# Attention inside a four-layer kernel: one projection per turn, its halves swapped by DMA, and the maxima turned by 128 stationary columns

## The reference

```python
def _rope(q, k, seq_len, head_dim):
    ...
    def rot(t):
        t = t.reshape(*t.shape[:-1], half, 2)
        t0, t1 = (t[..., 0], t[..., 1])
        r0 = t0 * cos - t1 * sin
        r1 = t1 * cos + t0 * sin
        return jnp.stack([r0, r1], axis=-1).reshape(*t0.shape[:-1], head_dim)
    return (rot(q), rot(k))
B, S, _ = x.shape
H, D = (NUM_HEADS, HEAD_DIM)
qkv = x @ qkv_w + qkv_b
...
q, k = _rope(q, k, S, D)
scale = math.sqrt(D)
attn = jnp.einsum('bhqd,bhkd->bhqk', q, k) / scale
attn = jax.nn.softmax(attn, axis=-1)
out = jnp.einsum('bhqk,bhkd->bhqd', attn, v)
out = jnp.transpose(out, (0, 2, 1, 3)).reshape(B, S, H * D)
return out @ out_w + out_b
```

## Time and profile before

| | us |
|---|---|
| median of 3 timed runs | 1847.09 |
| lowest, highest | 1846.87, 1849.22 |
| the profiled execution, its own time | 1842.65 |
| its span, first to last instruction | 1840.8 |
| TensorE busy | 1729.1 (94%) |
| VectorE busy | 1443.2 (78%) |
| GpSimd busy | 1430.2 (78%) |
| ScalarE busy | 1408.2 (76%) |

### The profile page before, as it was taken

One profiled execution on the slowest core, in us unless ns is written; L12 is line 12 of the kernel. 1 busy time (PEld: TensorE's weight loads), 2 busy tenths in 40 slices (PEclk: granted clock), 3 DMA queues, 4 the chain that ended last, 5 costly groups with the idle time before them and its releaser, 6 DMA issues. The chain is left out here.

```text
span 1840.8 us, 54091 instructions
## 1 busy us (share of the span) xinstructions
PE 1729.1 (94%) x22916; PEld 1097.3 (60%) x22916; DVE 1443.2 (78%) x2658; ACT 1408.2 (76%) x1737; POOL 1430.2 (78%) x851
## 2 busy tenths in 40 slices
PE   5999999999999999999999999986899999978997
PEld 2466666666666666666666666675566666653454
DVE  5888888888888888888888887525988888855785
ACT  2688888888888888888888889943898888853463
POOL 6699999999999999999999999974765566634122
PEclk9899999999999999999999999998999999999998
DMA  5101010101010110101010100041121111110000
GB/s 143 25 20 31 19 31 22 28 24 30 22 29 24 26 30 20 30 24 28 23 31 19 28 19 11 2 149 28 42 45 37 37 37 37 33 26 0 1 0 24
DMA packets 71080, 56.89 MB, mean 31 GB/s; under 512 B 29196, under 2 KB 64184, under 8 KB 70840
## 3 DMA queue, kind: packets, MB, share of 16 engines
q1 hardware_dynamic: 70840, 53.44, 11.5%
HBM read 14.54 MB, written 1.05 MB: 8 GB/s over the span
## 5 line engine op out<-in xcount | busy, mean ns | idle before, releaser
L278 POOL TENSOR_TENSOR ah_probs_lo<-ah_probs,ah_probs_hi 128x1024 f16<-128x1024 f32 x512 | 1072.6, 2133 | 79.4 <-ACT ah_probs L487 79.2
L542 DVE TENSOR_REDUCE ah_part_max<-ah_p_m 128x1 f32<-128x512 f32 x1024 | 668.6, 685 | 121.7 <-PE ah_p_m L342 111.4
L484 ACT ACTIVATE ah_probs_hi<-ah_p_s 128x1024 f16<-128x1024 f32 x512 | 531.2, 1038 | 190.1 <-PE ah_p_s L358 178.9
L487 ACT ACTIVATE ah_probs<-ah_p_s 128x1024 f32<-128x1024 f32 x512 | 532.5, 1040 | 0.0
L372 PE MATMUL ah_p_o<-ah_v_hi,ah_probs_hi 128*128 128x65 f16 x4096 | 470.3, 194 | 5.7 <-POOL ah_probs_lo L278 5.1
L374 PE MATMUL ah_p_o<-ah_v_lo,ah_probs_hi 128*128 128x64 f16 x4096 | 470.3, 193 | 0.0
L376 PE MATMUL ah_p_o<-ah_v_hi,ah_probs_lo 128*128 128x65 f16 x4096 | 470.1, 194 | 0.0
L372 PEld LDWEIGHTS ah_p_o<-ah_v_hi,ah_probs_hi 128*128 128x128 f16 x4096 | 382.8, 98 | 84.2 <-DVE a_attn L565 12.3
L374 PEld LDWEIGHTS ah_p_o<-ah_v_lo,ah_probs_hi 128*128 128x128 f16 x4096 | 378.3, 98 | 91.4
L342 PE MATMUL ah_p_m<-ah_k_hi_lo,ah_q_hi_twice 128*128 128x512 f16 x1024 | 393.6, 385 | 7.1 <-DVE ah_part_max L542 3.7
L357 PE MATMUL ah_p_s<-ah_q_hi_twice,ah_k_hi_lo 128*128 128x512 f16 x1024 | 388.7, 380 | 0.8 <-ACT ah_probs L487 0.4
(11 more groups left out here) (318 smaller groups left out, 3074.9 us busy)
## 6 DMA issues: line engine op xcount, KB each, us to landing
ba_v_skew<-ba_v_own SPq DMA_DIRECT2D x64, 129.0 KB, 2.3
ah_q_hi_twice<-ah_hi SPq DMA_DIRECT2D x128, 64.0 KB, 2.0
ah_k_hi_lo<-ah_hi SPq DMA_DIRECT2D x64, 64.0 KB, 1.9
ah_one_k_hi<-ah_hi SPq DMA_DIRECT2D x64, 64.0 KB, 2.0
ah_k_hi_lo<-ah_lo SPq DMA_DIRECT2D x64, 64.0 KB, 2.0
ah_max_q_lo<-ah_lo SPq DMA_DIRECT2D x64, 64.0 KB, 2.0
ah_w_head<-in_w_heads SPq DMA_DIRECT2D x16, 160.0 KB, 2.4
bw_rot<-in_rot SPq DMA_DIRECT2D x4, 512.0 KB, 8.1
```

Source lines behind the costliest of these rows:

```text
L278: pool.tensor_tensor(pl[:, p % RW, :, :], pb[:, p % RP, :, :], ph[:, p % RW, :, :], ALU.subtract).then_inc(lo_pool, 1)
L484: act.activation(ph[:, p % RW, :, :], p_s[:, p % 2, :, :], ACT.Exp, scale=HD ** -0.5)
L487: act.activation(pb[:, p % RP, :, :], p_s[:, p % 2, :, :], ACT.Exp, scale=HD ** -0.5).then_inc(exp_done, 1)
L542: dve.tensor_reduce(part[:, t, 2 * half + b:2 * half + b + 1], p_m[:, b, :], AX, ALU.max).then_inc(maxed, 1)
```

## The change

Before, the loop projected q and k twice a turn, once with the halves of each head exchanged. Now it projects once, with `W_QK`, in step 0. VectorE multiplies this result with the sine into a new tile `half` (`times_sin`), and SP's queue copies its four blocks of 32 partitions into `rot`, each to its neighbour's place (four transfers of 64 KB, semaphore `swapped`). The table's sine has opposite signs in the two halves, so what was an addition becomes a subtraction (`minus_swapped`). This stands in step 3, where `high` stood; `high` and `low` both stand in step 4. The projections ahead of the loop stay as they were, and so the weights are put in another order: from the third head on only 192 of 320 columns are loaded and split. `neg_max` is widened to 128 columns, of which 124 are zero, so that `turn_max` has 128 stationary columns and writes 128 rows, of which four are used.

```diff
-W_TURNED, W_QK, W_V = slice(2 * HD, 4 * HD), slice(0, 2 * HD), slice(4 * HD, 5 * HD)
+W_QK, W_V, W_TURNED = slice(0, 2 * HD), slice(2 * HD, 3 * HD), slice(3 * HD, 5 * HD)
+W_LATER = 3 * HD
...
+        half = sc.sb("sin_part", [P, CH])
...
-        negm = sc.sb("neg_max", [P, TPC], F16)
+        negm = sc.sb("neg_max", [P, P], F16)
...
+        SWAP = 4 * 16
+        HALF_A = HD // 2
...
-                        sp.dma_start(w32[:, :], a["w_heads"][h + 1]).then_inc(w_in, 16)
+                        sp.dma_start(w32[:, 0:W_LATER], a["w_heads"][h + 1][:, 0:W_LATER]).then_inc(w_in, 16)
+                    if g >= LEAD_G:
+                        sp.wait_ge(sin_done, g - LEAD_G + 1)
+                        sp.wait_ge(r_done, g)
+                        for b in range(4):
+                            sp.dma_start(rot[(b ^ 1) * HALF_A:((b ^ 1) + 1) * HALF_A, :],
+                                         half[b * HALF_A:(b + 1) * HALF_A, :]).then_inc(swapped, 16)
...
-                    pool.tensor_copy(wh[:, h % 2, :], w32[:, :]).then_inc(w_hi_done, 1)
+                    cols = slice(0, W_COLS if h * QC < LEAD_G else W_LATER)
+                    pool.tensor_copy(wh[:, h % 2, cols], w32[:, cols]).then_inc(w_hi_done, 1)
...
-                    pe.matmul(p_a[0:TPC, 0:P], negm[:, :], identh[:, :], start=True, stop=True).then_inc(m_turned, 1)
+                    pe.matmul(p_a[:, 0:P], negm[:, :], identh[:, :], start=True, stop=True).then_inc(m_turned, 1)
...
                     if j == 0 and g <= LAST_G:
                         pe.wait_ge(vl_done, g)
-                        project(turned_bank(g), g, W_TURNED, turned_ready)
-                    if j == 1 and g <= LAST_G:
-                        pe.wait_ge(rot_done, g + 1)
                         project(proj_bank(g), g, W_QK, proj_ready)
...
+                def times_sin(g):
+                    h, c = divmod(g, QC)
+                    dve.wait_ge(proj_ready, g + 1)
+                    if g > LEAD_G:
+                        dve.wait_ge(swapped, SWAP * (g - LEAD_G))
+                    dve.scalar_tensor_tensor(half[:, :], proj_bank(g), bqk[:, 0, h:h + 1], sin[:, chunk(c)], ALU.add,
+                                             ALU.mult).then_inc(sin_done, 1)
...
+                def minus_swapped(g):
+                    dve.wait_ge(cos_done, g + 1)
+                    dve.wait_ge(swapped, SWAP * (g - LEAD_G + 1))
+                    dve.tensor_tensor(proj_bank(g), proj_bank(g), rot[:, :], ALU.subtract).then_inc(r_done, 1)
...
-                    dve.tensor_reduce(negm[:, :], part[:, :, :], AX, ALU.max, negate=True).then_inc(m_done, 1)
+                    dve.tensor_reduce(negm[:, 0:TPC], part[:, :, :], AX, ALU.max, negate=True).then_inc(m_done, 1)
...
+                dve.memset(negm[:, :], 0.0).then_inc(negm_zeroed, 1)
...
                         if j == 0:
-                            rotate_sin(g)
+                            times_sin(g)
                         if j == 1:
+                            dve.wait_ge(sin_done, g - LEAD_G + 1)
                             rotate_cos(g)
-                        if j == 2:
-                            rotate_sum(g)
                         if j == 4:
-                            low(g)
+                            high(g)
...
                         if j == 3:
-                            high(g)
+                            minus_swapped(g)
+                        if j == 4:
+                            low(g)
```

More of the change, by code:

```diff
@@ L175, in mha_heads @@
          vl_done, m_ready, maxed, m_done, m_turned, mrow_ready, s_ready, exp_done, lo_pool, o_ready, rcp_done,
-         o_free, wo_in, bias_turned, bias_done, biased, evac_t, evac_p) = (sc.sem(n) for n in (
+         o_free, wo_in, bias_turned, bias_done, biased, evac_t, evac_p, sin_done, swapped,
+         negm_zeroed) = (sc.sem(n) for n in (
              "ident_in", "w_in", "bias_in", "x_turned", "xh_ready", "xl_ready", "v_ones", "zeroed", "consts",
@@ L180, in mha_heads @@
              "mrow_ready", "s_ready", "exp_done", "lo_pool", "o_ready", "rcp_done", "o_free", "wo_in",
-             "bias_turned", "bias_done", "biased", "evac_t", "evac_p"))
+             "bias_turned", "bias_done", "biased", "evac_t", "evac_p", "sin_done", "swapped",
+             "negm_zeroed"))
         x_in = [sc.sem(f"x_in{c}") for c in range(NCH)]
@@ L238, in split_weights @@
                         pool.wait_ge(v_ready, QC * (h - 1))
-                    pool.tensor_copy(wh[:, h % 2, :], w32[:, :]).then_inc(w_hi_done, 1)
+                    cols = slice(0, W_COLS if h * QC < LEAD_G else W_LATER)
+                    pool.tensor_copy(wh[:, h % 2, cols], w32[:, cols]).then_inc(w_hi_done, 1)
                     pool.wait_ge(w_hi_done, h + 1)
-                    pool.tensor_tensor(wl[:, h % 2, :], w32[:, :], wh[:, h % 2, :], ALU.subtract).then_inc(w_split, 1)
+                    pool.tensor_tensor(wl[:, h % 2, cols], w32[:, cols], wh[:, h % 2, cols],
+                                       ALU.subtract).then_inc(w_split, 1)
                 split_weights(0)
@@ L546, in negate_max @@
                     dve.wait_ge(maxed, 2 * PAIRS_A * (e + 1))
+                    if e == 0:
+                        dve.wait_ge(negm_zeroed, 1)
                     if e >= 1:
                         dve.wait_ge(m_turned, e)
-                    dve.tensor_reduce(negm[:, :], part[:, :, :], AX, ALU.max, negate=True).then_inc(m_done, 1)
+                    dve.tensor_reduce(negm[:, 0:TPC], part[:, :, :], AX, ALU.max, negate=True).then_inc(m_done, 1)
                 def max_rows(e):
@@ L2303, in _layouts @@
     turned = np.roll(order, HD // 2)
-    a["w_heads"] = c(np.concatenate([w[:, 0][..., order], w[:, 1][..., order], w[:, 0][..., turned],
-                                     w[:, 1][..., turned], w[:, 2]], -1).transpose(1, 0, 2))
+    a["w_heads"] = c(np.concatenate([w[:, 0][..., order], w[:, 1][..., order], w[:, 2],
+                                     w[:, 0][..., turned], w[:, 1][..., turned]], -1).transpose(1, 0, 2))
     b = i["L0_attn_qkv_b"].reshape(3, HEADS, HD)
```

## The result

The changed kernel takes 1803.36 us, median of 4 runs (1800.33 to 1808.95), against 1846.98 (1846.11 to 1849.22). The ratio is 0.9767, with a 95% interval of 0.9742 to 0.9792. The profiled execution took 1800.95 us with a span of 1799.0.

What follows compares the result with a forecast made beforehand. TensorE's list was taken to bound the loop, GpSimd next. Terms of -0.65, -0.12 and +0.15 gave -0.62 us a turn, 18.20 to 17.58; over 58 turns -36.0, so 1847.1 became 1811 us, range 1803 to 1817 (chance 0.60).

Steps and rivals of the forecast that it cites:

- What bounds the loop: Loop with projections: TensorE's list sets 18.20 us a turn; GpSimd would stop the fall at about 16.7.
- The second projection: Step 1 on TensorE: dropping this projection saves its whole slot, -0.65 us a turn, since nothing hides it.
- The wait of the maximum in step 3: TensorE, step 3: with the addition gone from step 2, VectorE is earlier and the wait goes, -0.12 us a turn.
- The turning, and the wait for `lo_done`: Turning matmul on TensorE: waits 0.33 us for `low`, +0.15 us a turn net of the saving there; bounds -0.18 and +0.45.
- The width of `neg_max`: At the turning: a 128-column load would be made ahead, saving up to 0.18 us a turn; bounds -0.18 and 0.
- Rival (c): At the turning: the stall comes from its semaphores and 0.09 stays; -0.53 us a turn, 1816 us; chance 0.08.
- The swap: Four DMA transfers on SP's queue: land before the subtraction with slack 2.2 us, at worst 0.7; cost 0.
- Rival (e): Swap transfers run one behind the other, the last 1.9 us late: +1.28 us a turn, 1921 us, slower; chance 0.04.
- GpSimd: Splitting a head's weights there is off the path; its need is at most 17.0 us a turn, under 17.6.
- Rival (d): GpSimd and ScalarE hold the loop; if GpSimd keeps 1.0 us idle, 18.0 a turn, 1835 us; chance 0.07.
- Rival (a): At the turning: no wait for `lo_done`, VectorE's steps 3 and 4 being earlier; -0.95 us a turn, 1792 us; chance 0.12.
- Rival (b): Steps 3 to 5: VectorE's chain becomes the bound, 0.3 us more felt; -0.32 us a turn, 1829 us; chance 0.09.

Runs made afterwards that it cites:

- e3: Kernel before with the loop's second projection taken out, nothing moved and the exchange of halves left out: turn 17.63 us, median 1814.97 us, ratio 0.9834.
- e1: Kernel before with only `neg_max` and its turning load widened to 128 columns: turn 18.01 us, median 1833.39 us, ratio 0.9937.
- e2: Changed kernel with the turning load back to 4 columns: turn 17.55 us, median 1807.59 us, ratio 0.9797 to the kernel before.
- e8: Changed kernel without the four swap transfers, the subtraction reading `half` unexchanged: turn 17.49 us, 1806.88 us (one run).
- e7: Changed kernel with four small copies issued on SP's queue ahead of the swap, making it late: turn 18.35 us, 1857.83 us (one run).
- e5: Changed kernel with the subtraction at the end of step 2, `high` in step 3, `low` at the front of step 4: turn 17.48 us, 1804.04 us, ratio 0.9765.
- e9: Changed kernel with the turning matmul and its `lo_done` wait moved behind step 5's second weighing on TensorE: turn 17.31 us, 1794.67 us, ratio 0.9718.
- e4: Changed kernel with `high` behind the subtraction in step 3 and `low` at the front of step 4: turn 17.71 us, 1817.47 us, ratio 0.9845.

## Why the prediction was right, and where it was off

The forecast was 1811 us and a turn of 17.58; it came to 1803.4 and 17.48. That is the fast edge of the range that was given (1803 to 1817), and one misread term, below, carries it there.

- **What bounds the loop.** TensorE's list before, with GpSimd at about 16.7 behind it. Both held: TensorE is still busy for 969.6 of 972.4 us in the loop, and the last turns stayed at 16.5.
- **The second projection, -0.65.** Alone it brought -0.57 (e3). Of the 0.08 that is missing, 0.05 went to GpSimd in the fourth turn and 0.03 to the maximum of step 3, so the price of the slot was right.
- **The wait of the maximum in step 3, -0.12.** It is gone: that maximum stands 0.03 behind the weighing (588.63 to 588.66), as the sum had it.
- **The turning, and the wait for `lo_done`, +0.15.** The mechanism was right, its size was not. The chain of VectorE was counted to the hundredth (2.49 us). The term that failed is the 0.12 between a waiting load and its matmul, taken from the load of a weighing: here load and matmul start together at 593.13. Those rows were misread. The matmul ahead of that weighing is a maximum of 512 columns, which started at 610.44 in the kernel before:

```profile
610.44 0.38 PE L342 MATMUL ah_p_m<-ah_k_hi_lo,ah_q_hi_twice 128*128 128x512 f16 x1
```

The next matmul can start 0.22 us later, at 610.66, and that is where the weighing stands: it waited for its turn on TensorE, not for its load. The earlier trace rows already showed the turning's load and matmul starting together, at 615.50. So the place costs +0.04 instead of +0.15. At 58 turns these 0.11 us are 6.4, and the end of the turns with projections moved by 41.9 us where 36.0 were forecast, 5.9 more. The rest of the 7.6 us between forecast and result is no larger than what executions of one kernel differ by.
- **The width of `neg_max`.** Worth 0.19 by itself (e1), as the upper bound of the prediction had it, and 0.07 within the change (e2). Rival (c), a stall that comes from the semaphores, fell with e1.
- **The swap, 0.** Right: no cost (e8), landings of 2.0 us in the median, a slack of 2.2 us (e7) and 0.7 at worst, as counted. Rival (e), the late swap, is a real mechanism: e7 is slower than the kernel before (18.35 us a turn against 18.20). Its condition, four transfers one behind the other, did not come. The prediction did not see that landings are late over a long stretch of the loop; the changed kernel has slack for it, e5 had not.
- **GpSimd.** Its need was taken as under 17.6 and so without cost. On the mean that is so, but not in the turn behind a split: 0.14 there, 0.035 on the mean, 2 us. Its 17.0 is a mean over four turns; the 0.94 us of a split fall into one. Rival (d) was right that GpSimd would hold the loop back, for another reason than it gave, and by little.
- **Rival (a)**, no wait at all, was reached only by moving the turning (e9). **Rival (b)**, VectorE's chain as the bound, is what e4 ran into.

With the two terms that the runs corrected the sum is -0.65 - 0.12 + 0.04 + 0.035 = -0.70, and -0.72 was measured. The 0.02 between them is not explained.

## What to carry to other kernels

When the bound engine has no idle time, price an edit by the distance between the starts of instructions, and then look who is next: here a second engine stood 8% behind and took back a twentieth of the gain through one turn in four. When an operation is inserted in a chain between two engines, move the wait on the waiting side behind work that does not need it (e9, one line) before reordering the chain (e4, no gain; e5, a gain only in the turns whose transfers landed early). A transfer on a loop's path needs slack for its late landings (here up to 3.7 us), not for the median one (2.0), and a look at landings over the whole loop, not in one turn. And before the distance between a waiting load and its matmul is taken as a cost, look at what the engine was doing in it.

## What was not expected of the hardware

- A matmul with 4 stationary columns cost 0.19 us more in the stream than one with 128 (turns of 18.20 and 18.01, before and e1).
- Transfers of one shape do not land alike all through an execution. In the changed kernel the median landing of the swap was 2.0 us up to 320 us, 2.4 between 356 and 848 us, and the longest 3.7. In e5 the late ones lie between 353 and 815 us (2.4 in the median, up to 3.4), in e7 issues or landings are late from the first turns on to about 900 us (landings of the swap up to 3.5, single issues up to 2.00 where the median is 0.59). No run tells what slows them.
- Four copies of 32 partitions by 64 bytes took SP's queue as long to issue as four of 32 by 2048 bytes, 2.44 and 2.49 us in an even turn of e7.
- The part of the kernel that the change does not touch is not equally long in each execution. From 1160 us to the end, with the last turning at 1147.3 to 1147.7 in each, three profiled executions of the changed kernel and its variants:

```profile
1160.00:1795.00 635.00, 550.75 (x6502) 357.59 (x6498) 462.95 (x946) 434.91 (x703) 322.76 (x293) 0.96 0.14 36
...
1160.00:1805.00 645.00, 561.64 (x6502) 365.00 (x6498) 464.65 (x946) 434.90 (x703) 322.66 (x293) 0.94 0.14 35
```

It took 635 us at a mean granted clock of 0.96, 639 at 0.96 in the first trace of the changed kernel, and 645 at 0.94 without the swap. A single total can so be off by 10 us, more than most terms of the sum, while the turn was the same to 0.01 us.
